# Attention scores on Trainium2: three PSUM banks for the exponential and two for the maximum, where it was two and three

## The reference, cut to what matters

```
for i in range(4):                       # 8 heads of 16 features
    q, k, v = heads(x @ Wq[i] + bq[i]), heads(x @ Wk[i] + bk[i]), heads(x @ Wv[i] + bv[i])
    scores = einsum('bhqd,bhkd->bhqk', q, k) / sqrt(16)
    attn = softmax(scores, axis=-1)
    o = merge(einsum('bhqk,bhkd->bhqd', attn, v)) @ Wo[i] + bo[i]
    x = layernorm(x + o, g1[i], be1[i])
    x = layernorm(x + relu(x @ W1[i] + b1[i]) @ W2[i] + b2[i], g2[i], be2[i])
```

## Time and profile before

| | |
|---|---|
| median of 3 runs | 1398.8 us (1398.34 to 1399.44) |
| the profiled execution | 1406.68 us, its span 1404.9 us |
| mean granted TensorE clock in it | 0.884 |
| first stage: first M item to last product of AV | 60 to 623 us |
| last stage: first M item to the end | 1292 to 1401 us |
| reductions at line 538 in both stages | 320, about 0.68 us each |
| exponentials at line 432 in both stages | 320, about 0.60 us each |

### The profile page before, as it was taken

One profiled execution on the slowest core, in us unless ns is written; L12 is line 12 of the kernel. 1 busy time (PEld: TensorE's weight loads), 2 busy tenths in 40 slices (PEclk: granted clock), 3 DMA queues, 4 the chain that ended last, 5 costly groups with the idle time before them and its releaser, 6 DMA issues. The chain is left out here.

```text
span 1404.9 us, 20748 instructions
## 1 busy us (share of the span) xinstructions
PE 1079.1 (77%) x7046; PEld 731.5 (52%) x7046; DVE 713.2 (51%) x1989; ACT 602.5 (43%) x1321; POOL 346.4 (25%) x336
## 2 busy tenths in 40 slices
PE   1467788868886888873588999996989898944677
PEld 1134454545554545542377576674677776832344
DVE  3355566656665667633645211114454445556654
ACT  3134444434553455441643613325545454541355
POOL 4313444444443444234601100013000003013110
PEclk9668899989998999996678989998999999965699
DMA  2745344524462446002000001100000000006640
GB/s 46 138 82 78 66 73 72 100 49 82 74 107 51 73 80 111 10 2 52 10 1 1 15 24 30 30 20 1 8 8 11 4 15 23 1 1 103 100 78 25
DMA packets 76093, 65.33 MB, mean 47 GB/s; under 512 B 11324, under 2 KB 73176, under 8 KB 75992
## 3 DMA queue, kind: packets, MB, share of 16 engines
q1 hardware_dynamic: 72968, 62.09, 24.8%
q0 software_dynamic: 512, 1.05, 0.5%
q10 hardware_dynamic: 2520, 0.99, 0.4%
HBM read 46.83 MB, written 17.27 MB: 46 GB/s over the span
## 5 line engine op out<-in xcount | busy, mean ns | idle before, releaser
L538 DVE TENSOR_REDUCE t_nmax<-banks 128x2 f32<-128x512 f32 x256 | 167.7, 682 | 72.6 <-PE banks L296 71.0
L432 ACT ACTIVATE t_probs<-banks 128x512 f32<-128x512 f32 x256 | 146.6, 597 | 107.2 <-PE banks L320 96.9
L320 PE MATMUL banks<-t_packed 99*128 99x256 bf16 x512 | 107.3, 294 | 34.4 <-issue 17.4
L296 PE MATMUL banks<-t_packed 96*128 96x256 bf16 x512 | 109.9, 302 | 25.4 <-DMA t_packed<-t_qk_parts 25.4
L320 PEld LDWEIGHTS banks<-t_packed 99*128 99x128 bf16 x512 | 45.8, 103 | 86.1 <-issue 63.4
L1824 ACT ACTIVATE l_probs<-banks,l_nmax 128x256 f32<-128x256 f32 x128 | 59.5, 470 | 69.5 <-DVE l_nmax L1850 69.5
L377 PE MATMUL banks<-x1T,wff 128*128 128x512 f32 x128 | 72.2, 675 | 18.5 <-ACT t_oT L442 17.6
L333 PE MATMUL banks<-t_probs,t_v 128*32 128x256 f32 x1024 | 84.7, 411 | 0.1
L1591 ACT ACTIVATE hid<-banks,b 128x512 f32<-128x512 f32 x64 | 43.5, 687 | 81.2 <-PE banks L1529 81.1
L1613 DVE SCALAR_TENSOR_TENSOR acc<-banks,gates,acc 128x128 f32<-128x128 f32 (+1 forms) x72 | 20.0, 342 | 108.8 <-PE banks L1547 108.8
L296 PEld LDWEIGHTS banks<-t_packed 96*128 96x128 bf16 x512 | 52.7, 106 | 42.0 <-DMA t_packed<-t_qk_parts 26.8
(11 more groups left out here) (346 smaller groups left out, 2289.1 us busy)
## 6 DMA issues: line engine op xcount, KB each, us to landing
t_packed<-t_qk_parts SPq DMA_DIRECT2D x192, 128.0 KB, 4.8
t_qk_parts<-t_parts SPq DMA_DIRECT2D x32, 384.0 KB, 6.0
g_packed<-g_qk_parts SPq DMA_DIRECT2D x48, 128.0 KB, 4.6
w<-in_L_ffn_w SPq DMA_DIRECT2D x16, 256.0 KB, 2.7
g_qk_parts<-g_parts SPq DMA_DIRECT2D x8, 384.0 KB, 5.8
wff<-in_L_tok_W SPq DMA_DIRECT2D x8, 256.0 KB, 3.2
bc<-in_tok_rows SPq DMA_DIRECT2D x4, 320.0 KB, 3.6
l_wqk<-in_l_qk SPq DMA_DIRECT2D x8, 128.0 KB, 2.0
```

Of the source, the lines that this page charges most:

```text
L296: ins = pe.matmul(m.mbank[:, n % 3, i * S:(i + 1) * S], m.packed[0:MROW, 0, g % PAIRS, h, c + qt * P:c + (qt + 1) * P], m.packed[0:MROW, 1 ...
L320: ins = pe.matmul(m.sbank[:, n % 2, i * S:(i + 1) * S], m.packed[0:MROW + 3, 1, g % PAIRS, h, c + kt * P:c + (kt + 1) * P], m.packed[0:MRO ...
L432: act.activation(m.probs[:, n % 6, :], m.sbank[:, n % 2, :], ACT.Exp).then_inc(sem["probs_ready"], 1)
L538: dve.tensor_reduce(m.nmax[:, b % 2, u // 4, 2 * hp:2 * hp + 2], m.mbank[:, n % 3, :].rearrange("p (i k) -> p i k", i=2), AX.X, ALU.max, n ...
```

## The change

Bank 2 moves from the M items to the S items. M item n now goes to bank n % 2 of two and waits for the reduction of item n - 2; S item n goes to bank n % 3 of three and waits for the exponential of item n - 3. ScalarE's and VectorE's reads follow. On no engine does an instruction move or come or go; only the counts in these two waits of TensorE differ.

```diff
-                    if n >= 3:
-                        pe.wait_ge(sem["max_taken"], n - 2)
+                    if n >= 2:
+                        pe.wait_ge(sem["max_taken"], n - 1)
                     for i in range(2):
                         h = 2 * (u % 4) + i
-                        ins = pe.matmul(m.mbank[:, n % 3, i * S:(i + 1) * S],
+                        ins = pe.matmul(m.mbank[:, n % 2, i * S:(i + 1) * S],
...
-                    if n >= 2:
-                        pe.wait_ge(sem["probs_ready"], n - 1)
+                    if n >= 3:
+                        pe.wait_ge(sem["probs_ready"], n - 2)
                     for i in range(2):
                         h = 4 * hq + 2 * hp + i
-                        ins = pe.matmul(m.sbank[:, n % 2, i * S:(i + 1) * S],
+                        ins = pe.matmul(m.sbank[:, n % 3, i * S:(i + 1) * S],
...
-                    act.activation(m.probs[:, n % 6, :], m.sbank[:, n % 2, :], ACT.Exp).then_inc(sem["probs_ready"], 1)
+                    act.activation(m.probs[:, n % 6, :], m.sbank[:, n % 3, :], ACT.Exp).then_inc(sem["probs_ready"], 1)
...
                     dve.tensor_reduce(m.nmax[:, b % 2, u // 4, 2 * hp:2 * hp + 2],
-                                      m.mbank[:, n % 3, :].rearrange("p (i k) -> p i k", i=2),
+                                      m.mbank[:, n % 2, :].rearrange("p (i k) -> p i k", i=2),
...
-    m.sbank = banks[:, 0:2, :]
-    m.mbank = banks[:, 2:5, :]
+    m.sbank = banks[:, 0:3, :]
+    m.mbank = banks[:, 3:5, :]
```

## The result

The changed kernel takes 1413.9 us in the median of 12 runs (1408.7 to 1417.4), against 1399.6 us of the kernel before beside it: a ratio of 1.0094, 95% interval 1.0074 to 1.0114. The prediction said 1395.3 us and at most 1402.0. The profiled execution took 1413.29 us, its span 1411.5 us, at a mean granted clock of 0.869 where it was 0.884.

A forecast was written before the change was run, and what follows sets the result against it. TensorE's in-order queue was taken to set the pace; clock falls -5.2, waits at L296 +1.1, early falls +0.5 and last stage +0.1 gave -3.5 us, from 1398.8 to 1395.3 us, 8-in-10 range 1391.5 to 1402.0.

The forecast's parts named there:

- rival 2: Whole kernel slower: the clock falls more often in places without cover, three odd steps net more; 1405.6 us, chance 0.15.
- Even steps, cost 0: In nine even steps M(2) moves by about 0.8 us, covered by the transposes' 0.95 us wait: cost 0.
- M(3) in the odd steps: Scores for the maximum, u = 3, wait 1.0 us for a reduction; the feed-forward wait swallows 0.65, keeping 1.1.
- The last layer's odd step: There M(3) waits some 0.8 us for a reduction, with a cover of 0.1: +0.7 us.
- Last stage as a whole: Chosen attention at the end: +0.7 us for a later M(4) and S(5), -0.15 and -0.45 at L320, together +0.1.
- Three of four late falls go, -5.2 us: Largest term: odd steps' clock falls behind the 1.76 us feed-forward wait, 1.7 us each; three expected to go.
- In a step of short cover: Odd steps: the clock falls more often at M(1), the transposes and M(3); +0.5 us over three such steps.
- The gain at L320, -0.6 us: Last stage, third bank for the exponential's scores: -0.15 us at S(7), -0.45 at S(2) of the final sequence.

## Why the prediction was wrong

The mechanisms were named; two numbers in the largest term failed, and rival 2, with 0.15, is what happened.

- **Even steps, cost 0**: right. The wait came out at 0.74 us, the step at 13.52 us.
- **M(3) in the odd steps**: right, 1.0 us of delay expected, and M(3) starts 1.04 us later in the step (4.98 against 3.94), of which 0.79 us are its own wait; with the clock up, the feed-forward wait keeps 1.14 us, forecast 1.1. The last layer's odd step went from 16.49 to 16.99 us: +0.5 against +0.7. Last stage as a whole, from its first S on: 98.35 us before, 98.20 after, against +0.1; but other executions, of before too, have 101 to 102 us there, so it is not tested at this size.
- **Three of four late falls go, -5.2 us**: mis-sized, since the starting point was wrong. They do go (none in the changed kernel), but a second execution of the kernel before has one and not four. I had seen that the profiled execution was 7.9 us above the median and took the count from it all the same, then subtracted its falls from the median. By the second execution the term is at most 1.7 us.
- **"In a step of short cover": +0.5 us for the early falls**: this step failed. I priced an early fall by the one at 341.79, which cost 0.06 us, one fall with 1.76 us of cover behind it. The same change that adds waits at M(1) and M(3) also takes 0.65 us of that cover, and the falls became double: TensorE works 3.0 us longer in the step (18.34 against 15.35), and only 1.5 us of that fit into its idle time. Seven of nine steps go to 20.2 to 20.5 us, where 19.0 stand without: 7 x 1.4 = 10 us. Rival 2 had this as "if the low clock that follows reaches past the cover"; its price of up to 1.7 us a step holds (1.4 measured), its count of three net was too low.
- **Where the loss lies.** Between the profiled executions of the changed kernel and the second one of the kernel before (9.8 us of span), the 18 steps from number 5 to 10 of the three turns take 303.1 against 294.0 us: 9.1 of the 9.8. The last odd step of the third turn adds 1.6 and three steps of the last layer 1.8. From the layer's last step on, where the change touches little but the last attention, the changed kernel is 5.1 us shorter (794.6 against 799.7), and the kernel before in its first execution shorter by 3.0 us than in its second: differences of this size a single profile can't place here.
- **The gain at L320, -0.6 us**: of the size that can't be measured, as was forecast. The Trainium skill, page "Perfetto Trace Analysis", section "Matmuls", advises to rotate independent groups through the banks; which of two sides should have one bank more it doesn't say. Here both rotate before and after the change, and 20 us of idle time taken away at L320 bought 0.2% by the two ratios, which their intervals can't tell from nothing.

The section of the Trainium skill that stood on rival 2's side is borne out. The Trainium skill, page "TensorE: Matmul & The Clock Gate", section "A second HAM failure mode: psum-queue depth-cycling", tells of short idle times between groups that cycle through banks, which make the clock swing. The runs agree: with waits of 0.84, 0.56 and 0.79 us and matmuls between them the clock fell in all nine steps, with the first or the third of them filled in three or four, with both filled in none.

## What to carry to other kernels

Price a new wait on TensorE twice: once as delay, against the cover behind it, and once as a trigger of the clock, against what is left of that cover after the first. A fall that cost nothing in the trace before was paid by idle time which the change may itself spend. Before a count of falls is used in a sum, take it from more than one execution; a profile well above the median is a warning. And where several short waits stand close together, filling or removing just one of them can be enough. Added matmuls are free only where the wait is as long as they are and no later delay needs it as its cover.

## What the runs showed of the hardware

- No single long wait is needed for the clock to fall: three of 0.84, 0.56 and 0.79 us, within 4 us, do it in nine steps of nine, in two kernels, and the low clock then lasts 6.8 us in most. In the kernel before it fell behind a wait of some 1.76 us, with one of 1.58 us 6 us ahead of it, in four of nine steps in one execution and in one of nine in the next.
- Unused matmuls in a wait shortened a step by 1.5 us although TensorE had more to do (18.82 against 20.30 us in the mean of nine).
- With twelve added matmuls in some odd steps TensorE stood 2.6 and 3.2 us elsewhere, at the start of a turn of the loop, with 57 instruction packets in place of 54; with six longer ones there were 54 packets and gaps of 0.67 us.
- The same store of the maxima, from its issue to the issue of the load that waits for it, took 4.85 to 6.97 us, and the steps that wait for it are longer or shorter by just that.
